# A three-layer graph network: the unit list and the first node features made in one interleaved phase, with a 0/1 product instead of a row gather

## What is computed

```python
h = maximum(layernorm(x), 0)                       # first phase: node features
h_edge = (h[src] + edge_attr) @ W                  # first layer, two heads
s = leaky(h_edge . attn_l + (h @ W) . attn_r [dst])
alpha = softmax of s over the edges of each dst
ft = segment_sum(h_edge * alpha, dst); mean of heads; batch norm; relu
x = x + ft
h = maximum(layernorm(x), 0)
for W, a_s, a_d, b in 3 layers:                    # plain layers
    hw = h @ W
    e = leaky((hw . a_s)[src] + (hw . a_d)[dst])
    h = segment_sum(softmax_dst(e) * hw[src], dst) + b   # relu between layers
out = x + h
```

## Time and profile before

| | us |
|---|---|
| median of three runs | 9480.21 |
| profiled execution | 9480.92 |
| its span in the trace | 9479.2 |
| first phase, from the start to the first transfer of the heads layer | 228.42 |
| DVE busy over the span | 7034.2 (74%) |
| POOL busy over the span | 6767.6 (71%) |
| PE busy over the span | 4772.3 (50%) |

### The profile page before, as it was taken

How to read it: one execution, slowest core, us unless ns; L and a number is a source line. 1 busy time by engine, 2 the same in 40 slices (tenths; PEclk the granted TensorE clock), 3 DMA queues, 4 the chain that set the end, 5 groups by cost and what they waited for, 6 DMA issues and landing times. The chain is left out here.

```text
span 9479.2 us, 125330 instructions
## 1 busy us (share of the span) xinstructions
PE 4772.3 (50%) x23674; PEld 4371.0 (46%) x23674; DVE 7034.2 (74%) x11845; ACT 4623.3 (49%) x12210; POOL 6767.6 (71%) x6888
## 2 busy tenths in 40 slices
PE   4677777777634444444444444444444444444434
PEld 4666666666623444444443444444443333333333
DVE  2788888888747777777776777777776777777777
ACT  1677777777614444444443444444443444444443
POOL 0777777777507777777776777777776777777776
PEclk9666666666655555555555555555555555555555
DMA  1222222222211111111111111111111111111111
GB/s 41 57 56 55 54 56 56 55 54 57 51 56 31 31 31 31 31 31 31 31 31 27 31 31 31 31 31 31 31 31 28 32 32 33 32 33 32 32 32 30
DMA packets 675574, 360.05 MB, mean 38 GB/s; under 512 B 549773, under 2 KB 550477, under 8 KB 675022
## 3 DMA queue, kind: packets, MB, share of 16 engines
q0 software_dynamic: 220896, 237.06, 13.3%
q1 hardware_dynamic: 454626, 122.45, 6.3%
HBM read 335.55 MB, written 23.35 MB: 38 GB/s over the span
## 5 line engine op out<-in xcount | busy, mean ns | idle before, releaser
L1323 POOL DMA_INDIRECT plain_rows_in<-table,plain_idx x5139 | 4965.9, 966 | 1590.7 <-issue 1590.7
L1571 PE MATMUL plain_ps_sums<-plain_rows_in,plain_prob 128*125 x10908 | 2435.1, 412 | 7.7 <-ACT plain_prob L1534 7.7
L1571 PEld LDWEIGHTS plain_ps_sums<-plain_rows_in,plain_prob 128*125 128x125 f32 x10908 | 2374.8, 329 | 33.2 <-ACT plain_prob L1534 8.3
L789 POOL DMA_INDIRECT heads_rows_in<-h_in,heads_idx x1713 | 1782.5, 1041 | 532.5 <-issue 532.5
L1534 ACT ACTIVATE plain_prob<-plain_prob 128x2250 f32<-128x2250 f32 x300 | 623.6, 2079 | 1845.3 <-DVE plain_prob L1459 1845.3
L1592 PE MATMUL plain_ps_max<-ident,plain_column_max 128*125 128x128 f32 x300 | 173.0, 577 | 2530.0 <-DVE plain_column_max L1440 2530.0
L1592 PEld LDWEIGHTS plain_ps_max<-ident,plain_column_max 128*125 128x125 f32 x300 | 85.2, 284 | 2606.5 <-DVE plain_column_max L1440 2606.5
L1525 ACT ACTIVATE plain_score_sb<-plain_mask,plain_rows_in 128x125 f32<-128x125 f32 x1800 | 553.8, 386 | 1318.8 <-DMA plain_rows_in<-table,plain_idx 1318.8
L1434 DVE TENSOR_TENSOR plain_top<-plain_score_sb,plain_ps_score 128x750 f32<-128x750 f32 x300 | 280.9, 936 | 1149.5 <-ACT plain_ps_score L1525 1145.9
L1525 ACT ACTIVATE plain_ps_score<-plain_mask,plain_rows_in 128x125 f32<-128x125 f32 x3600 | 1059.0, 347 | 0.0
L1019 ACT ACTIVATE heads_masked<-heads_mask,heads_scores_sum 128x125 f32<-128x125 bf16 x3600 | 1052.1, 385 | 2.4 <-DVE heads_scores_sum L854 2.1
(11 more groups left out here) (240 smaller groups left out, 7604.2 us busy)
## 6 DMA issues: line engine op xcount, KB each, us to landing
plain_rows_in<-table,plain_idx POOLq DMA_INDIRECT x5139, 2.4
heads_edges<-in_edge_attr SPq DMA_DIRECT2D x104, 544.0 KB
heads_rows_in<-h_in,heads_idx POOLq DMA_INDIRECT x1713, 2.4
plain_own<-table SPq DMA_DIRECT2D x312, 32.7 KB
table<-plain_out_sb SPq DMA_DIRECT2D x200, 32.7 KB
n_x<-in_x SPq DMA_DIRECT2D x2, 3125.0 KB
plain_unit_int<-unit_ints SPq DMA_DIRECT2D x312, 0.0 KB
plain_idx<-in_src SPq DMA_DIRECT2D x312, 8.5 KB
```

Source lines behind the costliest of these rows:

```text
L789: gp.indirect_dma_start(rows_in[h][:, t, :], None, table[:, :], bass.IndirectOffsetOnAxis(ap=idx[h][:, t:t + 1], axis=0)).then_inc(done, 16)
L1323: gp.indirect_dma_start(rows_in[h][:, t, :], None, table[:, :], bass.IndirectOffsetOnAxis(ap=idx[h][:, t:t + 1], axis=0)).then_inc(done, 16)
L1571: ins = te.matmul(sums[h % 2], prob[h % 2][:, t, :], rows, start=t == 0, stop=t == Q - 1)
```

## The change

- `dst_next` goes; its first column alone is loaded (`dst_after`, 125 numbers), and the sorted test compares `dst_f` with itself shifted.
- The gather of L219 goes. The boundary row is picked by a product: `select` is 1 where a boundary lies in a row, and PE multiplies it with `dst_f`, four pieces of up to 512 columns through two PSUM banks; DVE compares each piece there.
- The three columns that are summed over the marks are split into five bf16 columns, and the marks are written as bf16 (`past`); 74 products remain, now in bf16.
- The layer norm is cut into steps (`LayerNorm`), which stand between the steps of the list on DVE. `x` is loaded in five chunks. The mean's scaling is folded into the subtraction.
- PE turns two blocks by one transpose (128 columns out of `xs`, before the ReLU, which ACT applies as it copies) and multiplies both by one product with an 8-column weight of two diagonal halves. Groups 0 to 11 stand ahead of the list products, the rest behind.
- SP stores chunks 0 to 3 of the nodes ahead of the list, chunk 4 behind it.
- In the heads layer unit 0 is loaded before the five weight transfers.

```diff
 def list_units(...)
             def _(sp):
-                sp.dma_start(dst_rows[:, :], rows_of(0)).then_inc(dst_loaded, 16)
-                sp.dma_start(dst_next[:, :], rows_of(1)).then_inc(dst_loaded, 16)
+                sp.dma_start(dst_rows[:, :], rows_from(0)).then_inc(dst_loaded, 16)
+                sp.dma_start(dst_after[:, :], rows_from(row_len)[:, 0:1], ...).then_inc(dst_loaded, 16)
                 nodes.load(sp)
+                nodes.store(sp, 0, nodes.chunks - 1)
                 sp.wait_ge(list_made, 6)
...
-                nodes.store(sp)
+                nodes.store(sp, nodes.chunks - 1, nodes.chunks)
             def _(gp):
-                gp.wait_ge(row_known, 1)
-                gp.indirect_dma_start(edge_row[:, :], None, dst[0:n_edges].rearrange("(p j) -> p j", p=rows),
-                                      bass.IndirectOffsetOnAxis(ap=row_of_i[:, 0:1], axis=0)
-                                      ).then_inc(rows_gathered, 16)
-                gp.wait_ge(rows_gathered, 16)
             def _(ve):
+                def find_rows():
+                    step(ve.tensor_copy(dst_f[:, :], dst_rows[:, :]))
+                    step(ve.tensor_copy(after_f[:, :], dst_after[:, :]))
+                    step(ve.tensor_scalar(below[:, :], thr_row[:, :], dst_f[:, 0:1], None, ALU.is_gt))
+                    step(ve.memset(below[0:1, :], 1.0), below_made)
+                    step(ve.tensor_scalar(below_after[:, :], thr_row[:, :], after_f[:, 0:1], None, ALU.is_gt))
+                    step(ve.tensor_tensor(select[:, :], below[:, :], below_after[:, :], ALU.subtract), select_made)
...
+                def count_smaller():
+                    for k, cols in enumerate(pieces):
+                        ve.wait_ge(selected, k + 1)
+                        step(ve.tensor_scalar(smaller[:, cols], ps_rows[k % 2][0:blocks + 1, 0:cols.stop - cols.start],
+                                              thr_col[:, 0:1], None, ALU.is_lt), piece_taken)
...
+                find_rows()
+                normal = LayerNorm(ve, nodes)
+                nodes.extend(ve)
+                normal.centre(0)
+                count_smaller()
+                normal.sum(0)
+                find_starts()
+                normal.centre(1)
+                count_units()
+                normal.scale(0)
+                mark_past()
+                for c in range(1, nodes.chunks):
+                    normal.sum(c)
+                    if c + 1 < nodes.chunks:
+                        normal.centre(c + 1)
+                    normal.scale(c)
+                write_list()
             def _(te):
+                te.wait_ge(select_made, 1)
+                for k, cols in enumerate(pieces):
+                    if k >= 2:
+                        te.wait_ge(piece_taken, k - 1)
+                    te.matmul(ps_rows[k % 2][0:blocks + 1, 0:cols.stop - cols.start], select[:, :], dst_f[:, cols]
+                              ).then_inc(selected, 1)
...
+                half = nodes.groups // 2
+                nodes.tensor(te, 0, half)
                 te.wait_ge(past_made, 1)
                 for c in range(per_part + 1):
-                    ins = te.matmul(ps_sums[:, 3 * c:3 * c + 3], unit_row[0:blocks - 1, ...],
-                                    steps[0:blocks - 1, :])
+                    ins = te.matmul(ps_sums[:, SUMS * c:SUMS * (c + 1)],
+                                    past[0:blocks - 1, c:c + (P - 1) * per_part + 1:per_part],
+                                    steps_split[0:blocks - 1, :])
                 ins.then_inc(units_summed, 1)
-                nodes.tensor(te)
+                nodes.tensor(te, half, nodes.groups + 1)
 class LayerNorm:
+    def centre(self, c):
+        ve.wait_ge(n.loaded[c], 16)
+        self.step(ve.tensor_reduce(mean, x, AX.X, ALU.add))
+        self.step(ve.scalar_tensor_tensor(x, bcast(mean, 2, D), -1.0 / D, x, ALU.mult, ALU.add), n.centred)
+    def sum(self, c):
+        ve.wait_ge(n.squared, c + 1)
+        self.step(ve.tensor_reduce(var, n.sq[:, n.cols(c), :], AX.X, ALU.add), n.summed)
+    def scale(self, c):
+        ve.wait_ge(n.rooted, c + 1)
+        self.step(ve.reciprocal(rstd, rstd))
+        self.step(ve.tensor_tensor(x, x, bcast(rstd, 2, D), ALU.mult), n.scaled)
 class FirstNodes:
+    def scalar(self, ac):
...
+        square(0)
+        root(0)
+        if self.chunks > 1:
+            square(1)
+        for c in range(self.chunks):
+            copy_rows(c)
+            for k in range(self.of_chunk):
+                g = c * self.of_chunk + k
+                copy_turned(g)
+                if g >= 1:
+                    copy_products(g - 1)
+                if k == 0 and c + 1 < self.chunks:
+                    root(c + 1)
+                if k == 2 and c + 2 < self.chunks:
+                    square(c + 2)
+        copy_products(self.groups - 1)
+    def tensor(self, te, first, last):
...
+                for j in range(GROUP // 2):
+                    b = g * GROUP + 2 * j
+                    ins = te.transpose(self.ps_t[g % 2][:, j * NB:(j + 1) * NB],
+                                       self.xs[:, b:b + 2, :].rearrange("p t d -> p (t d)"),
+                                       self.con.ident[0:NB, 0:NB])
...
+                for j in range(GROUP // 2):
+                    at = 2 * j * self.width
+                    ins = te.matmul(self.ps_o[(g - 1) % 2][0:NB, at:at + 2 * self.width],
+                                    self.h_t[(g - 1) % 2][:, j * NB:(j + 1) * NB], self.pair_w[:, :])
 def heads_layer(...), sync:
+                for h in range(RING):
+                    sp.sem_inc(stored[h], 32)
+                load_unit(0, 0, 0, False)
                 for half in range(2):
                     sp.dma_start(w_cols[half * D:(half + 1) * D, :], w_out).then_inc(w_loaded, 16)
...
-                for h in range(RING):
+                for h in range(1, RING):
                     load_unit(h, h, 0, False)
```

276 lines of the change are left out of this document (177 added, 99 removed).

## The result

The changed kernel takes 9343.24 us, the median of four runs (9340.91 to 9343.92). The kernel before took 9480.0 us beside it (9476.06 to 9481.56, four runs). The ratio is 0.9856, with a 95% interval of 0.9839 to 0.9873. The forecast was 9348 us, with a range of 9334 to 9374. One execution was profiled; it took 9340.91 us, and its span of 9339.1 is 140.1 us shorter than the one profiled before.

What follows compares the result with a forecast made beforehand. The first phase's chain was taken as the bound: gather wait, list products, node groups. The heads layer starting at 99 instead of 228.4 us (-129.4) and -3 within it gave -132.4 on 9480.9, a 9348 us median; range 9334 to 9374.

Steps and rivals of the forecast that it cites:

- the term of the groups' pace: First phase, node groups on PE: 1.50 us a group against 2.74 before, 36 us for twenty-four groups.
- the 3 us taken off for the heads layer: Heads layer: its end moves between +1.3 and -5.1 us with unit 0 loaded first; -3 taken.
- DVE's first cast: Start of the first phase: DVE begins at 11.8 us, after POOL's IOTA, 5.4 us gained by one copy of `dst`.
- marks done: First phase, DVE's list: marks end at 43.4 us, without the gather's 45.0 us wait and with 9.5 of layer norm between.
- groups' products go on: First phase, PE: group 1's product starts at about 45.8 us, once ACT's root has sum 1 from behind the marks.
- from there to the heads layer's first transfer: End of the first phase: from the list at 88 us to the heads layer's start at 99, four chunks stored earlier.
- the end of 10 us: Marks written as bf16: upper end of about 10 us at a two-tensor pass's pace, against 5.13 kept.
- the rival at 9351.5: List products at half an f32 record, 0.11 us each, 8.2 in all, 3.5 more than the term; chance 0.09.
- slow products: Rival: list products or marks stay slow through stride or type, +13 and +5 us, about 9366; chance 0.12.
- the fast rival: PE runs at the fast pace in groups and list products until DVE and ACT bound, near 9340; chance 0.08.
- the -5.1 end: Heads layer's best case: the remaining 6.4 us of DVE's waits for gathers won back by gathers that are ahead.
- the rival in which the layer wins nothing: Heads layer: DVE is late by 1.3 us and keeps it, 9352.5; chance 0.12.

Runs made afterwards that it cites:

- experiment 1: The changed kernel with list sums in f32 again (148 records, three columns, no bf16 split): 9399.19 us median, heads layer begins at 123.64 us.
- experiment 2: The changed kernel with one block of nodes per transpose and per product instead of two: 9401.09 us, heads layer begins at 126.56 us.
- Experiment 4: The changed kernel with the heads layer's weight transfers issued ahead of unit 0, as before the change: 9369.87 us, heads layer begins at 93.53 us.
- experiment 9: The kernel before with only the 0/1 product replacing the gather, and one copy of `dst`: ratio 0.9959, heads layer begins at 180.43 us.
- experiment 3: The changed kernel with all list steps up to the marks before the layer norm and list products before all groups: 9363.52 us, heads layer at 89.97.

## Why the prediction held, and where it did not

The forecast's mechanism held: the gather's wait went, the list products shrank, the groups took two blocks at a time, and the heads layer began so much earlier. The time came out 5 us lower than the forecast; the first phase alone is 5.2 us shorter than its sum, nearly all of it the term of the groups' pace, and the 3 us taken off for the heads layer are not shown. These are the steps against the trace.

| step | predicted | measured |
|---|---|---|
| DVE's first cast | 11.8 | 11.90 |
| marks done | 43.4 | 44.1 |
| longest DVE wait before that | under 2 | 1.41 |
| groups' products go on | 45.8 | 46.27 |
| 24 groups from there, without the list products | 36.0 | 31.0 |
| list products | 4.7 | 4.81 |
| PE free for the tails | 86.5 | 82.1 |
| list done | 88 | 83.5 |
| from there to the heads layer's first transfer | 11.1 | 10.2 |
| that transfer | 99 | 93.77 |
| first gather behind it | 7.8 | 7.55 |
| first use of gathered rows behind it | 35 | 34.4 |
| heads layer | -3 | -5.9 in the pair of traces, -2.1 in the medians |
| plain layers | 0 | within 1 |
| profiled execution | 9348.5 | 9340.91 |

**The gather.** Right in mechanism and size; alone, the product brings 48.0 us. The comparison from PSUM was priced at 0.7 us for 512 columns by the earlier trace rows; a pair of pieces took 1.54, 0.77 each; with the 164 columns of the last piece (1.18 less 0.77) that is 1.0 ns per element, as the earlier trace rows had it.

**The marks.** I kept 5.13 us for the bf16 output, without a row for it. The trace and experiment 1 show 5.13 for both types; the end of 10 us was never near.

**The list products.** The open question was a strided bf16 load. It took 0.065 us a record (4.81 by 74), by the scaled row of L1112 0.064. The Trainium skill, "TensorE: Matmul & The Clock Gate", section "Weight-path perf modes — Fast Weight Load (FWL) and DoubleRow", gives such a load about twice the pace; the forecast had priced that as half of an f32 record, 8.2 us in all. The trace shows less than a third of one, 0.065 against 0.24, so the rival at 9351.5 built on that pace falls, and so does that of slow products.

**The groups' pace: the term that was mis-sized.** I took 1.50 us a group: 0.55 for two transposes and 0.95 for four records with hand-over. It is 0.46 and 0.70, so 1.16 where PE runs through, and 1.29 over the 24 groups: ACT's passes of 1.27 us, which I had called just covered, leave PE standing 0.42 or 0.43 us six times, and it stands 1.33 once, at 50.28. The error of 5.0 us over the groups is nearly the first phase's difference of 5.2, 99 against 93.8; products that go on 0.5 late and an end that is 0.9 shorter make up the rest. The four product records are 0.175 us apart, where eight with 64 rows are 0.221 apart (experiment 2); I had taken 0.222 from a row with another shape, and then added a hand-over, which experiment 2 shows to be hidden. Why four records are cheaper one by one was not tried.

**The clock.** The forecast called the slow pace 1.2 GHz. It had that from the pace of the records, and the pace held; but the granted clock in the trace of the kernel before reads 1.00 over the whole first phase, the 148 records of 0.24 us included (the last section has the row).

**The range** does not follow from its own terms. 9480.2 less 129.4, less the 8.1 of the fast rival and less 5.1 is about 9338, not 9334; slow products and marks with a heads layer 1.3 longer give about 9370, not 9374. The measured time lies inside either.

**The rival of the fast pace** named 9340, close to the 9343.24 measured, but its mechanism is not what happened: the transposes of 125 columns stayed at 0.23 us apart and the list products at 0.065, both of the slow pace. A shorter group and the heads layer brought the time there instead.

**The heads layer.** I said that POOL's first gather would come 3.3 us earlier, and it comes 3.6 earlier; that the first use would be 1.3 late, and it is 0.6 late; and that DVE's remaining waits for gathers, 6.4 us, could be won back. In the pair of traces that looks right: 6.4 less 0.6 is 5.8, and 5.9 was measured. Experiment 4 took this apart. The first unit's wait returns when the weights go first, but the layer grows by 1.3 us in its trace and 1.8 in the medians, and the later waits, from 0 to 4.1 us with unit 0 first, change from run to run without it. The wait for gathers at the first unit, 17.92 us before, is replaced by one of 11.4 for ACT, as the two views of the line show; and one profiled execution of a pair is no measure of 5 us, since three kernels with the same heads layer on one chip differ by 1.9 there. So the -3 is not shown: what the runs give is between 0 and -2.1 in the medians, within their scatter. The reason for the -5.1 end was wrong, and on the second chip the rival in which the layer wins nothing is the one that fits. That -3 helped the total is luck.

**Where the 134.7 us come from.** By the experiments: the product 48.0 (done alone, with 5.4 of the single copy of `dst` in it), the bf16 parts 29.9 and two blocks per transpose 32.8 (each undone alone). Of the 24.0 that are left, 20.9 can be read from the rows, though no experiment isolates them. From the issue of the first store of `h_in` that stands behind the list to the heads layer's first transfer passed 30.2 us before, 198.22 to 228.42, and as long in experiment 9; it is 9.3 in the changed kernel, 84.49 to 93.77, where four of the five chunks are stored while PE still turns groups. The forecast had 21 for this. The other 3.1 are open; experiment 3 shows that the order in which list and node steps alternate is no part of it, since the kernel wins 3.8 us without it.

## What to carry to other kernels

When the work of two chains is interleaved by hand, look at what each inserted block holds up on the third engine: the 5 us of marks here cost nothing on DVE, yet held a sum, the sum held ACT's root, and the root held ACT's copies and with them PE. Price a repeated group by records of its own shape where double buffers exist, and count hand-overs only if a trace shows them; and do not read a few microseconds of a long layer from one pair of profiled executions, but from medians less the phase that is known, and only beyond the scatter of their runs. How the rows of a transfer are cut can decide how many DMA engines carry it, so the last store before a barrier deserves a look at its busy share.
